# A fused diffusion, attention and expert block on one core: the 32 token steps taken in another order, with the key and value store enlarged

## The reference, cut to what matters

```python
u = zX * lap_x(x) + zY * lap_y(x) + zR * x * (1 - x)      # x: (16, 256, 256), mirrored edges
hn = layernorm(u, ln1_w, ln1_b)
q, k, v = split(hn @ in_proj_w.T + in_proj_b)             # 16 heads of 16
scores = q . k / 4, causal over the first axis (16 long)  # s attends to t <= s
x1 = u + softmax(scores) @ v @ out_proj_w.T + out_proj_b
hn2 = layernorm(x1, ln2_w, ln2_b)
gates = the two largest of softmax(hn2 @ router_w.T), else 0      # 8 experts
y = sum over e of gates[e] * gelu(hn2 @ w1[e]) @ w2[e]            # 256 -> 512 -> 256
out = x + x1 + y
```

## Time and profile before

| | |
|---|---|
| median of 3 runs | 748.74 us (745.62 to 749.02) |
| the profiled execution | 748.15 us |
| its span, first to last instruction | 746.4 us |
| PE busy | 611.9 us, 82% |
| POOL busy | 456.7 us, 61% |
| DVE busy | 436.1 us, 58% |
| ACT busy | 353.0 us, 47% |

### The profile page before, as it was taken

How to read it: one execution, slowest core, us unless ns; L and a number is a source line. 1 busy time by engine, 2 the same in 40 slices (tenths; PEclk the granted TensorE clock), 3 DMA queues, 4 the chain that set the end, 5 groups by cost and what they waited for, 6 DMA issues and landing times. The chain is left out here.

```text
span 746.4 us, 10164 instructions
## 1 busy us (share of the span) xinstructions
PE 611.9 (82%) x2640; PEld 405.9 (54%) x2640; DVE 436.1 (58%) x1028; ACT 353.0 (47%) x817; POOL 456.7 (61%) x560
## 2 busy tenths in 40 slices
PE   2668897657657579879789999999699999999992
PEld 1334454335434446546556656667476676767671
DVE  1266899999599953646876589979944000011110
ACT  4343343131232236756666665656357555544440
POOL 6777676488744743687768866583375844444342
PEclk9998888587688789979979999999989999999997
DMA  4366653112311122243222433253244543444432
GB/s 122 120 223 193 206 154 105 44 58 80 87 43 38 33 60 44 58 111 70 50 57 52 87 57 50 39 97 56 36 87 80 123 75 66 65 72 67 65 54 26
DMA packets 51547, 59.83 MB, mean 80 GB/s; under 512 B 7386, under 2 KB 47075, under 8 KB 51428
## 3 DMA queue, kind: packets, MB, share of 16 engines
q0 software_dynamic: 18288, 23.28, 19.3%
q1 hardware_dynamic: 33204, 35.91, 16.7%
HBM read 35.89 MB, written 27.46 MB: 85 GB/s over the span
## 5 line engine op out<-in xcount | busy, mean ns | idle before, releaser
L433 POOL DMA_INDIRECT out_dram<-y,xin x71 | 117.4, 1653 | 42.9 <-issue 33.6
L966 PE MATMUL b_y<-w_s,hm_hmT 128*128 x568 | 135.0, 381 | 6.6 <-ACT y L535 5.8
L951 PE MATMUL b_h<-w_s,xT 128*128 x284 | 136.1, 602 | 1.6 <-ACT xT L496 1.6
L966 PEld LDWEIGHTS b_y<-w_s,hm_hmT 128*128 128x128 f32 x568 | 102.4, 190 | 20.0 <-issue 9.0
L1087 PE MATMUL b_at<-ident,pv_prod 128*128 128x128 f32 x544 | 79.2, 298 | 30.7 <-DVE pv_prod L897 30.7
L668 DVE TENSOR_SCALAR y<-b_y,xin,live 128x256 f32<-128x256 f32 x24 | 13.1, 544 | 141.8 <-PE b_y L966 141.8
L831 DVE TENSOR_TENSOR qk_prod<-q,kv 128x1024 f32<-128x1024 f32 (+2 forms) x80 | 88.1, 1125 | 5.0 <-ACT kv L565 4.2
L897 DVE TENSOR_TENSOR pv_prod<-kv,pr 128x1024 f32<-128x1024 f32 (+2 forms) x80 | 84.0, 1095 | 11.4 <-PE b_at L1087 11.3
L1087 PEld LDWEIGHTS b_at<-ident,pv_prod 128*128 128x128 f32 x544 | 70.6, 159 | 33.8 <-issue 32.5
L1043 PE MATMUL b_qk<-wqkv,hT 128*128 128x512 f32 x128 | 85.3, 802 | 0.0
L839 DVE TENSOR_REDUCE sc<-qk_prod 128x64 f32<-128x1024 f32 (+2 forms) x80 | 82.2, 1052 | 0.3
(11 more groups left out here) (166 smaller groups left out, 1045.7 us busy)
## 6 DMA issues: line engine op xcount, KB each, us to landing
xin<-xs_d SPq DMA_DIRECT2D x71, 132.5 KB, 2.1
w_s<-in_L_ffn_w_dram SPq DMA_DIRECT2D x16, 512.0 KB, 4.6
xp<-in_x_dram SPq DMA_DIRECT2D x32, 128.0 KB
xud<-in_x_dram SPq DMA_DIRECT2D x32, 128.0 KB
out_dram<-x POOLq DMA_DIRECT2D x32, 128.0 KB, 3.3
xud<-in_x_dram SPq DMA_DIRECT2D x32, 126.0 KB
out_dram<-y,xin POOLq DMA_INDIRECT x71
xud<-in_x_dram SPq DMA_DIRECT2D x64, 1.0 KB
```

Source lines behind the costliest of these rows:

```text
L433: pool.indirect_dma_start(out_rows, bass.IndirectOffsetOnAxis(ap=xin[:, j % NX, H:H + 1].bitcast(U32), axis=0), y[:, j % NY, :], None, com ...
L951: mm = pe.matmul(b_h[:, :], xT[:, k * P:(k + 1) * P], w1_s[:, bass.ds(e * (HC * F) + k * F, F)], start=(k == 0), stop=(k == HC - 1))
L966: mm = pe.matmul(b_y[:, 0:H], hmT[:, k * P:(k + 1) * P], w2_s[:, bass.ds(e * (FC * H) + k * H, H)], start=(k == 0), stop=(k == FC - 1))
```

## The change

The steps are taken in another order: positions 0 to 3 of the first half (g 0 to 3), positions 0 to 3 of the second (g 4 to 7), positions 4 to 15 of the first (g 8 to 19), positions 4 to 15 of the second (g 20 to 31). The second half's first four keys and values get rows of their own (`keys_at`, `values_at`; `kv` grows by eight rows), so that both halves' early keys are kept. From position 4 on the second half still overwrites the first half's rows, and the two guarding waits move from g = 16 to g = 20 (`AGAIN`). The groups of steps for the routing and their places g stay. `WANT` is written anew. To make room `zrow` is no longer a tile of its own but the last of the six input tiles of the slots, and the wait for the zero rows moves to the first load of that tile. The row numbers `idt` are made by four iotas where one stood.

```diff
+    FEW = 4
+    ORDER = [(c, p) for a, b in ((0, FEW), (FEW, S)) for c in range(B // P) for p in range(a, b)]
+    AGAIN = S + FEW
+    KV = S + FEW
...
-        zrow = sb("zrow", [P, ROW])
...
-        kv = sb("kv", [P, 2 * S, H])
+        kv = sb("kv", [P, 2 * KV, H])
...
+        zrow = xin[:, NX - 1, :]
...
-        WANT = [0] * 10 + [1, 1, 1, 2, 2, 2, 2] + [2, 1, 1, 1, 1, 1, 2, 2] + [2, 2, 2, 2, 2, 2, 2] + [1, 1, 1]
+        WANT = [0] * 13 + [2] * 7 + [1] * 2 + [2] * 10 + [1] * 3
...
-            for n in (PLACES if g != S else LATER)[WANT[g]]:
+            for n in (PLACES if g != AGAIN else LATER)[WANT[g]]:
...
-            return g > S
+            return g > AGAIN
...
-            return g // S, g % S
+            return ORDER[g]
+
+        def keys_at(g, t):
+
+            c, _ = ORDER[g]
+            return S + t if c and t < FEW else t
+
+        def values_at(g, t):
+
+            return KV + keys_at(g, t)
...
-                    if r == NG - 1:
-                        sp.wait_ge(s["pre_done"], 16 * E)
+                if j == NX - 1:
+                    sp.wait_ge(s["pre_done"], 16 * E)
...
-                if p == 0 and g > 0:
+                if g == AGAIN:
                     act.wait_ge(s["sc_ready"], g)
-                act.activation(kv[:, p, :], b_qk[:, H:2 * H], ACT.Copy).then_inc(s["qk_sb"], 1)
+                act.activation(kv[:, keys_at(g, p), :], b_qk[:, H:2 * H], ACT.Copy).then_inc(s["qk_sb"], 1)
...
-                if g == S:
-                    act.wait_ge(s["pv_piece"], PIECES[S - 1] + 1)
-                act.activation(kv[:, S + g % S, :], b_v[:, 0:H], ACT.Copy).then_inc(s["v_sb"], 1)
+                if g == AGAIN:
+                    act.wait_ge(s["pv_piece"], PIECES[AGAIN - 1] + FEW // TP + 1)
+                act.activation(kv[:, values_at(g, half_of(g)[1]), :], b_v[:, 0:H], ACT.Copy).then_inc(s["v_sb"], 1)
```

More of the change, by code:

```diff
@@ L165, in adaln_moe_block @@
         blo = pv_prod[0:1, 0, :].bitcast(F32R)
-        NPIECE = [(g % S) // TP + 1 for g in range(G)]
+        NPIECE = [p // TP + 1 for c, p in ORDER]
         PIECES = [sum(NPIECE[:g]) for g in range(G + 1)]
@@ L361, in later_constants @@
                             pool.iota(iota_i[:, TMAX + 3 * E:TMAX + 3 * E + 1], [[1, 1]], base=0, channel_multiplier=1),
-                            pool.iota(idt[:, :].rearrange("p (c s) -> p c s", c=G // S), [[P, G // S], [B, S]], base=0,
-                                      channel_multiplier=1)]
+                            *[pool.iota(idt[:, g:g + n], [[B, n]], base=p * B + c * P, channel_multiplier=1)
+                              for g, c, p, n in ((0, 0, 0, FEW), (FEW, 1, 0, FEW), (2 * FEW, 0, FEW, S - FEW), (AGAIN, 1, FEW, S - FEW))]]
                 links_of.append(pool.iota(iota_w[:, :].rearrange("p (a b) -> p a b", b=2), [[16, ALL // 2 + 1], [0, 2]],
@@ L366, in later_constants @@
                 link(links_of[-1])
-                link(pool.memset(zrow[:, :], 0.0))
+                link(pool.memset(zrow, 0.0))
                 pool.tensor_copy(iota_f[:, :], iota_i[:, :])
@@ L408, in prefix @@
                     pool.indirect_dma_start(xs_d, bass.IndirectOffsetOnAxis(ap=pre_row[:, e:e + 1], axis=0),
-                                            zrow[:, :], None).then_inc(s["pre_done"], 16)
+                                            zrow, None).then_inc(s["pre_done"], 16)
             def add_x1(g):
@@ L479, in scale @@
             def scale(g):
-                i, p = g % 2, g % S
+                i, (_, p) = g % 2, half_of(g)
                 if g == 0:
@@ L554, in exponentials @@
             def exponentials(g):
-                n = NH * (g % S + 1)
+                n = NH * (half_of(g)[1] + 1)
                 act.wait_ge(s["sc_ready"], g + 1)
@@ L559, in queries_keys @@
             def queries_keys(g):
-                p = g % S
+                p = half_of(g)[1]
                 act.wait_ge(s["qkv_ready"], g + 1)
                 act.activation(q[:, g % 2, :], b_qk[:, 0:H], ACT.Copy).then_inc(s["qk_sb"], 1)
-                if p == 0 and g > 0:
+                if g == AGAIN:
                     act.wait_ge(s["sc_ready"], g)
-                act.activation(kv[:, p, :], b_qk[:, H:2 * H], ACT.Copy).then_inc(s["qk_sb"], 1)
+                act.activation(kv[:, keys_at(g, p), :], b_qk[:, H:2 * H], ACT.Copy).then_inc(s["qk_sb"], 1)
             def values(g):
-                if g == S:
-                    act.wait_ge(s["pv_piece"], PIECES[S - 1] + 1)
-                act.activation(kv[:, S + g % S, :], b_v[:, 0:H], ACT.Copy).then_inc(s["v_sb"], 1)
+                if g == AGAIN:
+                    act.wait_ge(s["pv_piece"], PIECES[AGAIN - 1] + FEW // TP + 1)
+                act.activation(kv[:, values_at(g, half_of(g)[1]), :], b_v[:, 0:H], ACT.Copy).then_inc(s["v_sb"], 1)
             def odds(r):
@@ L599, in _ @@
                     act.activation(junk[:, 0:1], junk[:, 1:2], ACT.Gelu)
-                if g == S:
-                    values(S)
+                if g == AGAIN:
+                    values(g)
                 if 0 <= g + 1 < G:
                     queries_keys(g + 1)
-                    if g + 1 != S:
+                    if g + 1 != AGAIN:
                         values(g + 1)
@@ L802, in _ @@
             for g in range(-AHEAD, G + 3):
-                T = g % S + 1
+                T = ORDER[g][1] + 1 if 0 <= g < G else 0
                 def stats():
@@ L833, in multiply @@
                             q[:, g % 2, :].rearrange("p (o h) -> p o h", o=1).to_broadcast([P, t1 - t0, H]),
-                            kv[:, t0:t1, :], ALU.mult)))
+                            kv[:, keys_at(g, t0):keys_at(g, t0) + t1 - t0, :], ALU.mult)))
                     def add_up(m):
@@ L869, in _ @@
                 v = g - 1
-                T = v % S + 1
+                T = ORDER[v][1] + 1 if 0 <= v < G else 0
                 if 0 <= v < G:
@@ L897, in value_products @@
                         dve.tensor_tensor(pv_prod[:, at % NPV, 0:(t1 - t0) * H].rearrange("p (t n d) -> p t n d", n=NH, d=D),
-                                                kv[:, S + t0:S + t1, :].rearrange("p t (n d) -> p t n d", d=D),
+                                                kv[:, values_at(v, t0):values_at(v, t0) + t1 - t0, :].rearrange("p t (n d) -> p t n d", d=D),
                                                 pr[:, v % 2, 0:NH * T].rearrange("p (n t o) -> p t n o", t=T, o=1)[:, t0:t1, :, :].to_broadcast([P, t1 - t0, NH, D]),
@@ L1074, in _ @@
                 if 0 <= v < G:
-                    T = v % S + 1
+                    T = half_of(v)[1] + 1
                     if v >= 1:
```

## The result

The changed kernel takes 738.62 us (median of 4 runs, 737.4 to 739.71), the kernel before 748.88 (median of 4 beside it, 745.62 to 750.39). The ratio is 0.987, 95% interval 0.983 to 0.991.

A forecast was written before the change was run, and what follows sets the result against it. The bound was taken to change by stage: a PE and ACT circle in steps 4 to 7, DVE in 8 to 15 except POOL in 12, slots later. Terms summed to −10.0 us from 748.15, giving 738, range 724 to 752.

The forecast's parts named there:

- The light steps have a floor without a key in it: Steps 4 to 7: the circle through PE and ACT sets the pace, so 41.0 becomes 40 us, −1.0.
- The rival in which the clock eats the gain: Light steps: PE idles more at the low clock, six steps of 11.8 us; total 748, no change, chance 0.17.
- Steps 8 and 9: Eight keys fewer beside the first table, but step 8 meets the circle's floor: 28.5 for 35.1 us, −6.6.
- Steps 10 and 11: Keys alone give 22.4 us, but POOL's load and eight scatters hold them at 24: −5.9.
- Step 12, POOL's zero blocks: POOL's blocks and scatters last as before and DVE waits longer: 24.5 for 25.9 us, −1.4.
- Steps 13 to 15, twelve keys fewer at 0.94: DVE-bound before, twelve keys fewer, POOL close behind after: 51.5 for 62.3 us, −10.8.
- Steps 16 to 19, by the nearest rows: Priced from steps 26 to 29 plus 3.8 us for the guarded eviction: 84.5 for 70.9 us, +13.6.
- The slower rival: Steps 16 to 19: POOL falls behind and slots cost 3.0 us instead of 1.0; total 754, slower at chance 0.12.
- Steps 20 to 22, the moved guard on the values: Waits for product pieces and output product where overwriting now starts, one slot more: 54.5 for 44.5 us, +10.0.
- Steps 23 to 29: Steps 23 to 25 −3.7 us, from two slots fewer in step 25; 26 to the end −0.5, one queue less.
- The rule on the shared port: Steps 16 to 19: two-input DVE and GpSimd instructions exclude each other; up to 22 us more if POOL set the pace.
- The larger gain: Rival: floors don't hold and every step shortens by its keys, total 711; floors partly or wholly gone (below 728), chance 0.16.

The follow-up runs named there:

- e_weights_late: Changed kernel with the expert weights loaded in iterations 5 to 12 instead of 1 to 10; 741.07 us, ratio to before 0.991.
- e_warm: Changed kernel with 14 unused identity transposes added on PE in each of iterations 0 to 9; 731.01 us, ratio to before 0.978.
- e_keys8: Changed kernel with four more key rows, so no guard on the keys in iteration 19, and a ring of 12 places for 16; 737.61 us.
- e_split: Changed kernel with POOL's eight zero blocks spread, two in each of iterations 11 to 14; 731.28 us, ratio to before 0.980.
- e_no16: Changed kernel with no slot in iterations 16 to 19, two back in step 25 and 46 behind the loop; 758.28 us, ratio 1.014.
- e_old_want: Changed kernel's order of steps with the old kernel's list of slots; 742.27 us, ratio to before 0.994.
- e_vals8: Changed kernel with four more value rows, so step 20's values are evicted in iteration 19, and a ring of 12 places for 16; 734.01 us.

## Why the prediction was right, step by step

**The light steps have a floor without a key in it.** Right, and the step on which the small size of the gain rested: DVE's busy time in steps 4 to 7 fell by 12.3 us, from 35.1 to 22.8 (the forecast had 15.0 for the sixteen keys, priced as quarters of a full piece), and they took 41.3 us for 41.0. e_weights_late speaks against the load of x, and e_warm shows the circle and what the clock has in it. The rival in which the clock eats the gain didn't come in this execution: every turn took 10.3 us, where the rival had 11.8. That is in part luck. In the execution of e_keys8, with the same light steps, they took 45.6 us, so its mechanism is real and varies from one execution to the next.

**Steps 8 to 11, two terms mis-sized in opposite directions.** Steps 8 and 9 gave 10.5 us, not 6.6. The term took the eight keys off at 0.94 us and then put 0.9 on for the floor; but before, DVE had been busy for 34.1 us there and after for 21.9, 12.2 less, 4.7 more than eight keys cost by the mean. The traces show where: durations added up, products and sums of keys fell by 7.9 us, as forecast, but the same 43 instructions of the first table fell by 3.8 (11.1 to 7.4), and the rest by 1.2. Single instructions of the table had run much longer before: one product of 128x40 took 871 ns and takes 202 now. Before, POOL's additions and two scatters ran beside the long part (133.5 to 140.5); now POOL is idle there from 127.1 on. The forecast had the table at 6.8 us in both orders. That POOL is the cause was not tested by an edit.

Steps 10 and 11 gave 2.2, not 5.9: POOL, busy for 25.0 of 27.7 us, is the nearest to a bound, and DVE waits for its root once in each step:

```profile
142.87 0.89 DVE L672 TENSOR_SCALAR ring<-x,mv,rstd 128x256 f32<-128x256 f32 x1 [3.02 <-POOL rstd L406]
...
157.50 0.82 DVE L672 TENSOR_SCALAR ring<-x,mv,rstd 128x256 f32<-128x256 f32 x1 [3.02 <-POOL rstd L406]
```

I had seen it, and set it at 22 to 24 with "eight scatters" from its 19.7 us of before; but the timelines show four scatters in that stretch of before and six in that of after, since shorter steps 8 and 9 push two of them into steps 10 and 11. That POOL sets the pace there was read from its busy time and these waits and not tested by an edit.

**Step 12, POOL's zero blocks.** Right: 24.8 us, with DVE waiting 11.30, and e_split takes 7.6 us out of it.

**Steps 13 to 15, twelve keys fewer at 0.94.** Right within 1.2.

**Steps 16 to 19, by the nearest rows.** Right in the sum (85.4 for 84.5), not in its parts. I priced the guarded eviction at 3.8 us; DVE's wait behind it is 4.13, and 2.8 us come back without the guard (e_keys8). The slots are held back for much less than the 10.0 us of the scores. The timeline of ACT shows that it wasn't free to begin with:

```profile
305.02 0.38 ACT L575 ACTIVATE q<-b_qk 128x256 f32<-128x256 f32 x1 [1.31 <-PE b_v L1056]
308.44 0.38 ACT L578 ACTIVATE kv<-b_qk 128x256 f32<-128x256 f32 x1 [3.03 <-DVE sc L864]
```

q came only at 305.0, seven of the ten us into the step, since PE made it late. The slots of iteration 18 aren't the reason: without them (e_no16) q comes 6.8 us into the step all the same, behind the sums of the product pieces and the output product. The guard lasts 3.03 us. The missing 1 us and more is in step 18, which waits 4.17 us for PE with no guard near it: with two slots ahead of four pieces PE frees DVE's three buffers late on its own. The step takes 20.8 us with its two slots, 17.4 with one (e_old_want) and 18.5 with none (e_no16). The slower rival, 3.0 us a slot, is excluded by e_no16: 0.7.

**Steps 20 to 22, the moved guard on the values.** Right: 53.9 for 54.5, its two waits 6.59 and 7.70 us where I had 5 and 8.2, and e_vals8 takes the first away and leaves 2.81 of the second.

**Steps 23 to 29.** −5.2 for −4.2, otherwise placed: the empty place in step 25 gives 2.1 us in that step (21.2 to 19.1) and 4.7 in step 26 (18.7 to 14.0), and step 27 gives 2.2 back (20.8 to 23.0). With two slots in step 25, e_old_want has 20.6, 18.5 and 20.5 in these three. Steps 23 and 24 take 31.1 us together for 30.7 (23 falls by 3.3, 24 rises by 3.7).

**The rule on the shared port** changed nothing. POOL's second addition of du took 1802 ns at most here and 1805 before. The first (L397) took up to 3056 ns, at the start of step 27, beside two of DVE's products in a row, where before it took 1622 at most. Steps 16 to 19 held POOL busy for 54.4 of 85.4 us and it never set their pace: DVE's waits there are for PE alone, 9.6 us in all.

**The larger gain** (711) failed for the reasons given: the floors held. It took three edits at those very floors to come to 719.

**The total.** That it came out within 0.1 us of the sum (−10.1 for −10.0 in the spans) is luck: the terms of steps 8 and 9, 10 and 11, 23 to 25 and 26 to 29 were off by −3.9, +3.7, +1.9 and −2.9 us and cancel. What the forecast had right is which stretches give, which give nothing and which cost.

## What to carry to other kernels

Moving work against an overlap is priced stage by stage: from each stretch only what its bound engine loses comes back, and a stretch that waits for a circle of engines or for another queue gives next to nothing (here 12.3 us of DVE work left steps 4 to 7 and the time stayed). Before an order is changed, look for the stretches that no work of the moved kind fills; here the three floors (a clock that sank in PE's waits, one block of transfers in a queue, a guard on a buffer) were worth 19 us, twice the new order. The guard on the keys cost from the moment at which ACT would otherwise have been free, 3.0 us, not from the start of the 10.0 us of scores that it waits for.

## What the runs showed of the hardware

PE's clock can be held by work without a use. Fourteen transposes of 128 by 128 a step, 1.9 us placed in its waits, brought the granted clock of steps 4 to 7 from 0.83 to 1.00, the four wide matmuls from 3.68 to 1.98 us, and the turn shown from 10.35 to 8.65.

And the same code can run the circle at several paces. In the profiled execution of the changed kernel steps 4 to 7 took 10.3 us each, at a granted clock of 0.83. The kernel before alternated, between 9.5 us at 1.00 and 11.0 at 0.69, and between 8.65 and 11.8 by ACT's evictions of q. This isn't a property of the order of steps: e_vals8 has the new order and the same light steps, and there q came at

```profile
63.17 0.38 ACT L577 ACTIVATE q<-b_qk 128x256 f32<-128x256 f32 x1 [4.40 <-PE b_v L1053]
...
74.99 0.38 ACT L577 ACTIVATE q<-b_qk 128x256 f32<-128x256 f32 x1 [7.30 <-PE b_v L1053]
...
83.64 0.38 ACT L577 ACTIVATE q<-b_qk 128x256 f32<-128x256 f32 x1 [4.18 <-PE b_v L1053]
...
95.45 0.38 ACT L577 ACTIVATE q<-b_qk 128x256 f32<-128x256 f32 x1 [7.33 <-PE b_v L1053]
```

that is, in turns of 11.8 and 8.65 us, while e_keys8 had steps of 9.5, 11.0, 13.3 and 11.8. What decides the pace of an execution isn't shown. One profile of such a stretch can be 4 us from the next, so a small gain there needs more than one.
